# Attention in one kernel: two score banks and three banks for turned rows, instead of three and two

## The reference

```
xn = layernorm(x)                          # (32, 112, 256)
q, k, v = heads(xn @ Wq), heads(ctx @ Wk), heads(ctx @ Wv)     # 16 heads of 64
scores = einsum('bhnd,bhmd->bhnm', q, k) * 64 ** -0.5          # 112 x 375 for each b and h
attn = softmax(scores, axis=-1)
out = einsum('bhnm,bhmd->bhnd', attn, v)
x = x + tanh(g_xattn) * (concat(out) @ Wo + bo)
x = x + tanh(g_ffn) * experts(layernorm(x))                    # 14 routed (top 2), 2 shared
```

## Time and profile before

| | |
|---|---|
| median of 3 runs | 1512.32 us (1511.09 to 1512.71) |
| profiled execution | 1510.65 us, its span 1508.8 us |
| busy: PE, PEld, DVE, ACT, POOL | 96%, 89%, 72%, 64%, 28% |
| attention, first scores to last | 35.9 to 1041.7 us |
| start of scores to start of scores, from pair to pair | 63.7 us (pairs 1 to 14) |

### The profile page before, as it was taken

One profiled execution on the slowest core, in us unless ns is written; L12 is line 12 of the kernel. 1 busy time (PEld: TensorE's weight loads), 2 busy tenths in 40 slices (PEclk: granted clock), 3 DMA queues, 4 the chain that ended last, 5 costly groups with the idle time before them and its releaser, 6 DMA issues. The chain is left out here.

```text
span 1508.8 us, 32792 instructions
## 1 busy us (share of the span) xinstructions
PE 1444.3 (96%) x9774; PEld 1345.5 (89%) x9774; DVE 1083.5 (72%) x2632; ACT 960.9 (64%) x2417; POOL 415.7 (28%) x662
## 2 busy tenths in 40 slices
PE   6999999999999999999999999999599989999998
PEld 6899999999999999999999999998389978888888
DVE  4778788787888878778788787876586534444448
ACT  4777777777777777777777777775353335444452
POOL 1013133231323313233131432310100135555520
PEclk9999999999999999999999999999899999999999
DMA  4010311213111121211303113010512246653235
GB/s 121 6 36 30 112 71 47 78 46 107 75 47 74 50 104 51 75 71 53 104 23 103 71 53 104 14 69 13 195 65 112 78 163 231 242 197 125 78 117 219
DMA packets 55294, 136.93 MB, mean 91 GB/s; under 512 B 10481, under 2 KB 38145, under 8 KB 51649
## 3 DMA queue, kind: packets, MB, share of 16 engines
q1 hardware_dynamic: 48608, 118.01, 22.5%
q0 software_dynamic: 6624, 18.13, 3.8%
HBM read 86.69 MB, written 49.43 MB: 90 GB/s over the span
## 5 line engine op out<-in xcount | busy, mean ns | idle before, releaser
L651 ACT ACTIVATE prob<-bank,nmax 128x375 f32<-128x375 f32 x448 | 258.8, 578 | 182.2 <-DVE nmax L740 180.2
L740 DVE TENSOR_REDUCE nmax<-bank 128x1 f32<-128x375 f32 x448 | 241.2, 539 | 47.0 <-PE bank L514 46.2
L723 DVE TENSOR_TENSOR pT_lo<-bank,pT_hi 125x384 fp32r<-125x384 f32 x448 | 246.2, 549 | 32.1 <-ACT pT_hi L662 30.5
L570 PE MATMUL bank<-keep_ident,prob 128*125 128x128 f32 x1344 | 224.9, 276 | 24.0 <-DVE pT_lo L723 20.0
L570 PEld LDWEIGHTS bank<-keep_ident,prob 128*125 128x125 f32 x1344 | 198.3, 187 | 44.6 <-DVE pT_lo L723 20.7
L662 ACT CAST pT_hi<-bank 125x384 fp32r<-125x384 f32 x448 | 212.4, 474 | 2.1 <-PE bank L570 2.0
L512 PE MATMUL bank<-attend_wvo_hi,zT_hi 128*112 128x256 f32 x512 | 169.3, 331 | 0.6 <-DVE zT_lo L723 0.6
L512 PE MATMUL bank<-pT_hi,kv_hi 125*128 125x448 f32 x384 | 151.6, 395 | 1.2 <-DVE zT_lo L723 1.0
L513 PE MATMUL bank<-attend_kvT_hi,qp_lo 128*128 128x376 f32 x448 | 150.7, 336 | 0.0
L512 PE MATMUL bank<-attend_kvT_hi,qp_hi 128*128 128x376 f32 x448 | 150.4, 336 | 0.2 <-DVE attend_kvT_lo L723 0.2
L514 PE MATMUL bank<-attend_kvT_lo,qp_hi 128*128 128x376 f32 x448 | 148.9, 332 | 0.0
(11 more groups left out here) (245 smaller groups left out, 3707.1 us busy)
## 6 DMA issues: line engine op xcount, KB each, us to landing
w_split<-we_split SPq DMA_DIRECT2D x14, 2048.0 KB, 6.9
keep_weights<-w_split SPq DMA_DIRECT2D x14, 2048.0 KB
we_in<-in_w SPq DMA_DIRECT2D x28, 512.0 KB, 5.9
over_y_all<-y_rows SPq DMA_DIRECT2D x14, 512.0 KB, 9.6
kv_in<-in_ctx SPq DMA_DIRECT2D x32, 187.5 KB
h_rows<-hrow SPq DMA_DIRECT2D x32, 112.4 KB, 2.2
over_h_in<-h_rows SPq DMA_DIRECT2D x7, 514.0 KB, 6.3
x_in<-in_x SPq DMA_DIRECT2D x16, 224.0 KB, 2.9
```

The costliest lines, as they stand in the source:

```text
L570: last = nc.tensor.transpose(T[s % 2][0:MP, c * P:(c + 1) * P], prob[:, s % NB, c * MP:(c + 1) * MP], ident[:])
L651: nc.scalar.activation(prob[:, s % NB, :], score_bank(s)[:, 0:M], ACT.Exp, bias=nmax[:, s % NB:s % NB + 1], accum_out=psum_[:, s % NB:s % ...
L723: return nc.vector.tensor_tensor(dst, src, hi.bitcast(F32), ALU.subtract)
L740: nc.vector.tensor_reduce(nmax[:, s % NB:s % NB + 1], score_bank(s)[:, 0:M], AX, ALU.max, negate=True).then_inc(max_ready, 1)
```

## The change

One bank moves from the scores to the turned rows. `scores` of step g now waits for the exp of g - 2 at every step, and `turn` of tile g waits for `pT_lo` of tile g - 3 (g - 2 for tiles 1 and 27 of a pair). No instruction that computes is added, removed or moved on any engine. The whole diff:

```diff
@@ -243,8 +243,8 @@
         we_landed, we_step, we_stored, rms_landed = sem("we_landed"), sem("we_step"), sem("we_stored"), sem("rms_all_landed")
         WE_STEPS = 7
 
-        S = banks[0:3]
-        T = banks[3:5]
+        S = banks[0:2]
+        T = banks[2:5]
         Z, O, SIDE = banks[5], banks[6], banks[7]
         ident = sb["ident"]
 
@@ -298,7 +298,11 @@
 
         def score_bank(s):
 
-            return S[1 if s == STEPS - 1 else s % 3]
+            return S[s % 2]
+
+        def turn_bank_of(s):
+
+            return T[1 if s == STEPS - 1 else s % 3]
 
         def units_of(t):
 
@@ -553,7 +557,7 @@
                 if j == 0:
                     pe.wait_ge(side_lo, kv_job(p, b) + 1)
 
-                need(pe, exp_done, g - 1 if s in (1, STEPS - 1) else g - 2)
+                need(pe, exp_done, g - 1)
                 rows = slice(j * P, (j + 1) * P)
                 three(score_bank(s)[:, 0:MW], [qp[q][:, b, rows] for q in ("hi", "lo")],
                       [kvT[q][:, b, :] for q in ("hi", "lo")], True, True).then_inc(scores_done, 1)
@@ -565,9 +569,9 @@
                     pe.wait_ge(norm_act, STEPS // 2 * p + s // 2 + 1)
                 else:
                     pe.wait_ge(norm_dve, STEPS // 2 * p + s // 2 + 1)
-                need(pe, pT_lo, g - 1)
+                need(pe, pT_lo, g - 1 if s in (1, STEPS - 1) else g - 2)
                 for c in range(MC):
-                    last = nc.tensor.transpose(T[s % 2][0:MP, c * P:(c + 1) * P], prob[:, s % NB, c * MP:(c + 1) * MP],
+                    last = nc.tensor.transpose(turn_bank_of(s)[0:MP, c * P:(c + 1) * P], prob[:, s % NB, c * MP:(c + 1) * MP],
                                                ident[:])
                 last.then_inc(pT_done, 1)
 
@@ -659,7 +663,7 @@
                 g = steps(p, s)
                 act.wait_ge(pT_done, g + 1)
                 need(act, z_done, 8 * p + (P * (s - 6) - 1) // QUAD + 1)
-                nc.scalar.copy(pT["hi"][:, :, ring_place(s)], T[s % 2][0:MP, 0:MC * P].rearrange("p (c n) -> p c n", c=MC)
+                nc.scalar.copy(pT["hi"][:, :, ring_place(s)], turn_bank_of(s)[0:MP, 0:MC * P].rearrange("p (c n) -> p c n", c=MC)
                                ).then_inc(pT_hi, 1)
 
             def ctx_sums(p, qd):
@@ -751,7 +755,7 @@
 
             def turned(p, s):
                 dve.wait_ge(pT_hi, steps(p, s) + 1)
-                low(pT["lo"][:, :, ring_place(s)], T[s % 2][0:MP, 0:MC * P].rearrange("p (c n) -> p c n", c=MC),
+                low(pT["lo"][:, :, ring_place(s)], turn_bank_of(s)[0:MP, 0:MC * P].rearrange("p (c n) -> p c n", c=MC),
                     pT["hi"][:, :, ring_place(s)]).then_inc(pT_lo, 1)
 
             def ctx_sums(p, qd):
```

## The result

The changed kernel takes 1501.22 us, median of 4 runs (1500.38 to 1501.94); before it was 1512.51 us in 4 runs. The ratio is 0.9927, with a 95% interval from 0.9909 to 0.9944: 11.3 us faster. The prediction was 1500.5 us.

What follows compares the result with a forecast made beforehand. PE, busy 96% of the span, was taken as the bound, so gains come from its idle time: 4.1 + 6.6 + 0 + 1.0 = 11.7 us, 1499.0 us profiled, 1500.5 us as median; range 1495 to 1508 us.

Steps and rivals of the forecast that it cites:

- Where PE loses time: Stalls at the turns of steps 1, 15 and 21, 2.11 us a pair, as the cost of two turn banks.
- Step 1: turn(26) fills part of the stall, the sums behind it still wait for tile 24: 0.27 us gained, times 15.
- Steps 15 and 21: Stalls of turn(12) and turn(18) go, capped by scores(22) waiting for exp(20): 0.47 us together, times 14 pairs.
- exp(20) moves along: Rival: POOL's work starts earlier with PE, the cap at step 22 falls, 1497.5 us; chance 0.14.
- The price of the third score bank: Tighter exp wait of the scores: binds at step 22 past 0.55 us; pair 0 loses 0.5 us, gains as much.
- The end: Pair 15: turn(12) gives 0.3 us back, two later turns are alike, 1.0 us in all.
- Half a gain: Rival: step 1 earns 0 and step 15 half, as tile 10 comes late: 5 us, 1507 us; chance 0.12.
- Nothing: Rival: the data's wait replaces the turn's everywhere, within 2 us of 1512.3; chance 0.05.
- All of it goes: Rival: a third turn bank closes all three stalls, 32 us, 1480 us; chance 0.02.
- Slower: Rival: tile 18's scaling is held by POOL's second subtraction, delaying exp(20) and scores(22), 1535 us; chance 0.05.
- The hold by POOL: Tile 18's scaling on DVE, 1.58 us, is held by POOL's subtraction through the shared port lock.

Runs made afterwards that it cites:

- experiment 7: Kernel before, with ACT's table load of each pair moved behind the copy of tile 24's high part: 62.87 us from pair to pair, 1500.44 us.
- experiment 9: Kernel before, with tile 18 scaled by ACT instead of DVE: 63.34 us from pair to pair, 1509.27 us.
- experiment 5: Changed kernel, but only the turn of tile 26 waits for the tile three back, all others two back: 63.45 us from pair to pair, 1507.14 us.
- experiment 3: Changed kernel, but only the turns of tiles 12 and 18 wait three tiles back, all others two: 63.18 us from pair to pair, 1504.67 us.
- experiment 1: Changed kernel, but only the turn of tile 12 waits three tiles back, all others two: 63.71 us from pair to pair, 1510.83 us.
- experiment 4: Kernel before, with the scores of every step waiting for the exp two steps back, banks unchanged: 63.72 us from pair to pair, 1511.69 us.
- Experiment 8: Changed kernel, with tile 18 scaled by ACT instead of DVE: 62.76 us from pair to pair, 1499.38 us.
- experiments 8 to 10: Tile 18 scaled by ACT, on the changed kernel, the kernel before, and with only turn(12) waiting three back: 62.76, 63.34, 63.02 us a pair.

## Why the prediction was right

- **Where PE loses time.** Three stalls in a pair, 2.11 us together, for want of a turn bank: right as a reading of the trace, too simple as a cause. Two of the three have their root in an order or a port, and could be had without a bank: 0.82 us of the first by the table load's place (experiment 7), the third by the scaling's engine (experiment 9).
- **Step 1, 0.27 us.** Measured 0.24 us (experiment 5). The turn fills that much of the stall, and the sums wait for the same tile. The release took 0.13 us, where I had taken 0.14.
- **Steps 15 and 21, 0.47 us together, capped by exp(20).** Measured 0.52 us (experiment 3); the changed kernel has 0.51 us beside its step 1. The step that failed is a part of it: "the gain is 0.32 to 0.34 us" at step 15. On its own it is 0 (experiment 1). I had followed the held scaling only to exp(20), which the scores of step 22 await, and not to `pT_lo` of tile 16, which stands on the same queue and which the turn of step 21 awaits. With both turns eased, only the first of the two caps counts, so the sum came out right.
- **The price of the third score bank.** By itself nothing in the loop: experiment 4 shows 63.72 us. But once PE came earlier by more than the 0.55 us of slack at step 22, the tighter wait did bind there, as the sum had it. Experiment 8, which lets exp(20) end earlier, got 0.19 us a pair back. Pair 0 lost 0.5 us with the tight wait alone and 0.2 us in the changed kernel. I had taken a loss of 0.5 us and as much gained back.
- **The end.** Pair 15 got 1.15 us shorter, and its step 1 is in that; I had 0.27 + 1.0.
- **The rivals.** *exp(20) moves along*: it did not. In pair 3 it ended 0.71 us earlier than before, just as POOL's subtraction started 0.71 us earlier, and the scores of step 13 had already come 0.72 us earlier; of what PE gained at step 15 it got nothing. *Half a gain* and *Nothing* fall with experiment 5 and with 62.94 us. *All of it goes* falls with 0.9 us left at step 1. *Slower* would have needed the scaling to come later against POOL, and that did not move by more than 0.01 us.
- **The hold by POOL.** "The trace agrees" was said of the scaling of tile 18, and holds for it. It does not hold for every pair of instructions, as the last section shows: the scaling of tile 16 meets another instruction of POOL and is not held.

What stays open: I did not try to move POOL's work instead of DVE's, so whether another scaling would be caught then is not shown.

## What to carry to other kernels

Before a bank is given to the instruction that stalls, look at what stands right behind it on its queue: here most of the long stall only moved by one instruction, since the next one needed the same data. An engine's gains don't add up when two of its meetings hang on something that doesn't move with it; find what is pinned (here DVE's scaling, by a POOL instruction), and ease all the waits behind it, or unpin it. And the cheapest cure was an order: a fixed cost of 1.28 us put behind the instruction that others awaited brought 12 us.

## What the runs showed of the hardware beyond that

The time outside the attention was not the same from kernel to kernel, though nothing there was changed. From the last scores to the end it was 467.5 to 470.3 us over the profiled executions: 467.75 before, 469.66 in the changed kernel. The granted clock differs with it. Stretches of before, then of the changed kernel (times, then busy us and count of PE, PEld, DVE, ACT and POOL, granted clock, DMA share, GB/s); the second of each holds the same eight matmuls:

```profile
1060.30:1070.50 10.20, 2.77 (x13) 2.80 (x14) 1.65 (x4) 1.17 (x2) 3.19 (x15) 0.50 0.65 222
...
1217.50:1220.70 3.20, 1.88 (x8) 1.33 (x8) 0.42 (x1) 0.86 (x2) 0.94 (x1) 1.00 0.88 369
```

```profile
1047.80:1061.20 13.40, 4.11 (x18) 3.66 (x19) 3.47 (x7) 2.19 (x4) 3.75 (x18) 0.50 0.58 195
1208.20:1211.40 3.20, 2.69 (x8) 1.70 (x6) 0.00 (x0) 0.86 (x2) 0.23 (x1) 0.50 0.99 415
```

After the attention, where PE mostly waits for the tokens' DMA, the clock stands at the lower of its two levels, 1.2 GHz, for 10.2 us before and for 13.4 us in the changed kernel. Some 177 us behind the last scores the changed kernel has a further stretch of 3.2 us at that level, where the kernel before has the full clock in the same work. The first and last rows of that work, before and changed:

```profile
1217.55 0.49 PE L1507 MATMUL bank<-keep_weights,over_tile_hT_hi 128*128 x1 [1.97 <-issue]
...
1219.05 0.38 PE L1494 MATMUL bank<-keep_ident,keep_tile_in 128*128 128x128 f32 x2
```

```profile
1207.79 0.55 PE L1511 MATMUL bank<-keep_weights,over_tile_hT_hi 128*128 x1 [1.95 <-issue]
...
1210.27 0.63 PE L1498 MATMUL bank<-keep_ident,keep_tile_in 128*128 128x128 f32 x2
```

From the first to the last it is 1.50 us before and 2.48 us at the lower clock: 1.0 of the 1.9 us. The rest, 0.9 us, has come up by 58 us behind the last scores. The other kernels fit. The seven executions that have this later stretch took 469.07 to 470.32 us from the last scores to the end, the seven that don't have it 467.45 to 468.99 us. PE was idle for 1.95 us ahead of that work in one kernel and for 1.97 us in the other, so why the clock fell in one of them only is not shown. The 1.9 us, and the first scores' start 0.8 us later, are why the spans of the profiled executions differ by 8.7 us when the attention is 11.5 us shorter.

A scaling on DVE that reads and writes SBUF can be held for most of a POOL instruction: that of tile 18 took 1.58 us instead of 0.42, in each of 14 pairs, and ended 0.20 us behind POOL's subtraction. The Trainium skill, SBUF — State Buffer, section Who interferes with whom, says that the second comer is blocked for the whole instruction; these rows agree, and experiments 8 to 10 show what it cost PE. But in the same 14 pairs the scaling of tile 16 starts and ends inside another POOL instruction, the multiplication of the expert's weights (L476), and takes its usual 0.42 us. In pair 3 of the kernel before:

```profile
258.78 1.67 POOL L476 TENSOR_SCALAR we_in<-we_in,rms_e 128x512 f32<-128x512 f32 x1 [0.18 <-POOL rms_e L471]
...
259.56 0.42 DVE L749 TENSOR_SCALAR prob<-prob,prob_inv 128x375 f32<-128x375 f32 x1
```

So the rule did not hold for every instruction of POOL. Its casts (in experiment 1, above) and its subtractions held DVE here, its multiplication did not, and no run shows why.
